# Softmax attention in a fused network: values' products one step later, joins in the next tile, mask after the scores

## The reference

```python
q = (h @ wq).reshape(B, S, NHEADS, HEAD_DIM)
k = (h @ wk).reshape(B, S, KVHEADS, HEAD_DIM)
v = (h @ wv).reshape(B, S, KVHEADS, HEAD_DIM)
q, k = _rope(q, k)
...
scores = jnp.einsum('bqhd,bkhd->bhqk', q, k) / np.float32(np.sqrt(HEAD_DIM))
scores = jnp.where(causal[None, None], scores, jnp.float32(-1e+30))
attn = jax.nn.softmax(scores, -1)
o = jnp.einsum('bhqk,bkhd->bqhd', attn, v).reshape(B, S, NHEADS * HEAD_DIM)
x = x + o @ wo
```

## Time and profile before

| what | us |
|---|---|
| median of three runs | 3796.96 |
| lowest and highest | 3794.91 and 3799.11 |
| the profiled execution | 3797.79 |
| its span, first to last instruction | 3795.8 |
| L0 attention, in the trace | 107.3 to 388.0 |
| L2 attention, first and second | 1045.1 to 1711.0 and 2482.1 to 3149.0 |

### The profile page before, as it was taken

One profiled execution on the slowest core, in us unless ns is written; L12 is line 12 of the kernel. 1 busy time (PEld: TensorE's weight loads), 2 busy tenths in 40 slices (PEclk: granted clock), 3 DMA queues, 4 the chain that ended last, 5 costly groups with the idle time before them and its releaser, 6 DMA issues. The chain is left out here.

```text
span 3795.8 us, 55139 instructions
## 1 busy us (share of the span) xinstructions
PE 3275.2 (86%) x16736; PEld 2538.9 (67%) x16736; DVE 2467.2 (65%) x4877; ACT 1972.1 (52%) x3957; POOL 1694.4 (45%) x1293
## 2 busy tenths in 40 slices
PE   5778699569888889988996899888889987998979
PEld 4566577138666666666884799756666666886767
DVE  4668545765578778885556565368778885555554
ACT  3777443333367667774333333267667774334333
POOL 1666221652276666762221454267666662221111
PEclk8999899899999999999998899899999999999989
DMA  2000131433211111103320000010111102332222
GB/s 76 23 30 2 50 116 62 125 109 113 76 26 25 28 31 30 27 7 110 108 93 21 6 1 1 29 39 25 25 28 30 30 9 93 113 105 86 70 95 75
DMA packets 81187, 204.07 MB, mean 54 GB/s; under 512 B 17179, under 2 KB 20379, under 8 KB 80662
## 3 DMA queue, kind: packets, MB, share of 16 engines
q1 hardware_dynamic: 80774, 200.74, 17.1%
q10 hardware_dynamic: 144, 0.07, 0.0%
HBM read 170.86 MB, written 4.69 MB: 46 GB/s over the span
## 5 line engine op out<-in xcount | busy, mean ns | idle before, releaser
L1252 POOL TENSOR_TENSOR probs<-probs,row_inverse 128x640 f32<-128x640 f32 (+7 forms) x640 | 739.0, 1159 | 514.5 <-DVE row_inverse L1278 503.0
L541 PE MATMUL psUp<-xnT_part,weights_part 128*128 128x512 f32 x3456 | 834.7, 391 | 3.3 <-DVE hidden L694 2.6
L541 PEld LDWEIGHTS psUp<-xnT_part,weights_part 128*128 128x128 f32 x3456 | 651.6, 189 | 141.7 <-issue 4.0
L518 POOL TENSOR_TENSOR weights_part<-weights,weights_part 128x768 fp32r<-128x768 f32 x136 | 250.9, 1848 | 1010.2 <-ACT weights_part L597 1010.2
L1266 DVE TENSOR_REDUCE neg_max<-psS 128x1 f32<-128x640 f32 (+7 forms) x640 | 477.0, 745 | 143.5 <-PE psS L1156 141.4
L1293 DVE TENSOR_TENSOR probsT_part<-psT,probsT_part 128x512 fp32r<-128x512 f32 (+1 forms) x960 | 501.9, 550 | 78.0 <-ACT probsT_part L1235 68.9
L1219 ACT ACTIVATE probs<-psS,neg_max 128x640 f32<-128x640 f32 (+7 forms) x640 | 475.6, 743 | 144.5 <-DVE neg_max L1266 127.7
L1235 ACT ACTIVATE probsT_part<-psT 128x512 fp32r<-128x512 f32 (+1 forms) x960 | 441.0, 491 | 174.0 <-PE psT L1168 164.4
L1189 PE MATMUL psO<-probsT_part,v_parts 128*128 128x512 f32 x1440 | 443.0, 423 | 73.7 <-DVE probsT_part L1293 72.7
L1152 PE MATMUL psS<-k_part,q_parts 128*128 128x512 f32 (+1 forms) x960 | 410.6, 428 | 80.3 <-ACT probs L1219 45.1
L1168 PE MATMUL psT<-ident,probs 128*128 128x128 f32 x2880 | 439.0, 276 | 43.1 <-DVE probsT_part L1293 39.3
(11 more groups left out here) (315 smaller groups left out, 4825.6 us busy)
## 6 DMA issues: line engine op xcount, KB each, us to landing
gates<-gate_rows SPq DMA_DIRECT2D x136, 512.0 KB, 4.0
weights<-in_l_ffn SPq DMA_DIRECT2D x148, 384.0 KB, 4.4
qk_swapped<-qk_raw SPq DMA_DIRECT2D x384, 64.0 KB, 2.0
bc_broadcast<-bc_rows SPq DMA_DIRECT2D x32, 512.0 KB, 4.5
w_group<-in_l_wgroup SPq DMA_DIRECT2D x16, 384.0 KB, 3.2
q_whole<-q_steps SPq DMA_DIRECT2D x32, 128.0 KB
w_o_group<-in_l_wo SPq DMA_DIRECT2D x16, 256.0 KB, 2.8
rope<-in_l_rope SPq DMA_DIRECT2D x2, 1024.0 KB, 5.3
```

Of the source, the lines that this page charges most:

```text
L518: nc.gpsimd.tensor_tensor(w[1][:, j, :], wt[:, j, :], w[0][:, j, :].bitcast(F32), ALU.subtract).then_inc(w_split, 1)
L541: last = nc.tensor.matmul(psU[:, u % 2, g, :], wp[:, j, g * D + k * P:g * D + (k + 1) * P], xp[:, k, cols(half)], start=n == 0, stop=n == ...
L1252: self.nc.gpsimd.tensor_tensor(self.p[:, n % 4, 0:w], self.p[:, n % 4, 0:w], self.rinv[:, at:at + 1].to_broadcast([P, w]), ALU.mult).then_ ...
```

## The change

The values' products move from a tile's steps 0, 1, 2 to its steps 1, 2, 3, and inside a step they stand between scores and turns instead of behind the turns. The join moves from step 3 of a tile to step 0 of the next one (the last tile's stays in step 30). The output jobs move two steps later (6, 10, 14, 18, 22, 26, 29, 31), with two buffers for `oT`; one projection moves from step 10 to 11, a rounding from 15 to 16, a split from 14 to 13, and the handling of the next group's values from steps 28 and 31 to 29 and 30 (GpSimd) and from 29 to 30 (VectorE). The product that adds the mask comes behind both score products of its block instead of between them. In L0 the roundings of steps 4 and 6 move to 13 and 14, the one of step 12 to 15, and the splits with them.

```diff
-    def joins(self, s):
-
-        return s == 30 or (s > 0 and s % 4 == 3 and s < 31)
+    def joined(self, s):
+
+        if s == self.UNITS - 2:
+            return NT - 1
+        return s // 4 - 1 if s > 0 and s % 4 == 0 else None
...
+                diagonal = b == qt // 4
                 nc.tensor.matmul(out[:, 0:w], queries, keys[0][:, b * HALF:b * HALF + w], start=True, stop=False)
-                if b == qt // 4:
-                    diagonal = out[:, qt % 4 * P:(qt % 4 + 1) * P]
-                    nc.tensor.matmul(diagonal, self.ident16[:], self.mask16[:], start=False, stop=False)
                 done = nc.tensor.matmul(out[:, 0:w], queries, keys[1][:, b * HALF:b * HALF + w],
-                                        start=False, stop=True)
+                                        start=False, stop=not diagonal)
+                if diagonal:
+                    done = nc.tensor.matmul(out[:, qt % 4 * P:(qt % 4 + 1) * P], self.ident16[:], self.mask16[:],
+                                            start=False, stop=True)
...
-            if s < 0 or r == 3:
+            if s < 0 or r == 0:
                 return
             blocks = self.blocks(s)
-            lo, hi = (r // 2 if r != 1 else 0, (r + 1) // 2) if blocks == 1 else (
-                r * blocks // 3, (r + 1) * blocks // 3)
+            lo, hi = (0 if r == 1 else 1, 1) if blocks == 1 else ((r - 1) * blocks // 3, r * blocks // 3)
...
             scores(g, s + 8, last)
+            values(g, s, last)
             turn(g, s + 4, last)
-            values(g, s, last)
             self.hooks.pe_step(pe, g, s, last)
...
-            if self.joins(s):
-                dve.wait_ge(self.shifted, NT * g + s // 4 + 1)
+            q = self.joined(s)
+            if q is not None:
+                dve.wait_ge(self.shifted, NT * g + q + 1)
...
-    PROJECT = (1, 3, 5, 7, 10, 13)
-    OUTPUT = (4, 8, 12, 16, 20, 24, 28, 31)
+    PROJECT = (1, 3, 5, 7, 11, 13)
+    OUTPUT = (6, 10, 14, 18, 22, 26, 29, 31)
+    ROUND_AT = {6: (0,), 8: (1,), 10: (2,), 12: (3,), 16: (4,), 18: (5,)}
+    SPLIT_AT = {7: 0, 13: 2, 15: 3, 22: 4, 24: 5}
...
-            if q:
-                self.wait_filled(dve, g, self.OUTPUT[q - 1], self.last)
+            if q > 1:
+                self.wait_filled(dve, g, self.OUTPUT[q - 2], self.last)
...
-        return self.nc.vector.tensor_tensor(self.oT[64 * half:64 * half + 64, :, :], first, second, ALU.add)
+        return self.nc.vector.tensor_tensor(self.oT[q % 2][64 * half:64 * half + 64, :, :], first, second, ALU.add)
...
-    ROUND_AT = {4: (0, 1), 6: (2,), 12: (3,), 20: (4,), 22: (5,)}
-    SPLIT_AT = {6: 0, 8: 2, 14: 3, 22: 4, 24: 5}
-    FIRST_KEYS_AT = 6
+    ROUND_AT = {13: (0, 1), 14: (2,), 15: (3,), 20: (4,), 22: (5,)}
+    SPLIT_AT = {14: 0, 15: 2, 16: 3, 22: 4, 24: 5}
+    FIRST_KEYS_AT = 14
```

More of the change, by code:

```diff
@@ L1279, in step @@
             maximum(g, s + 8, last)
-            if self.joins(s):
-                dve.wait_ge(self.shifted, NT * g + s // 4 + 1)
+            q = self.joined(s)
+            if q is not None:
+                dve.wait_ge(self.shifted, NT * g + q + 1)
                 for half in range(2):
                     pick = lambda ap: ap.rearrange("p (k h w) -> p k h w", h=2, w=P)[:, :, half, :]
-                    done = self.hooks.keep(dve, g, self.tile(s), half, pick(self.psO[0:self.dv, :]),
+                    done = self.hooks.keep(dve, g, self.tile(4 * q), half, pick(self.psO[0:self.dv, :]),
                                            pick(self.shift[:]))
@@ L1425, in dve_step @@
             self.split_first_keys(dve, g + 1)
-        if s == 29:
+        if s == 30:
             self.split_values(dve, g + 1, 0, slice(1, NT))
@@ L1449, in __init__ @@
         self.wo = s.sb("w_o_group", [P, KD, D])
-        self.oT = s.sb("oT", [P, KD, P])
+        self.oT = [s.sb(f"oT{i}", [P, KD, P]) for i in range(2)]
         self.rot = s.sb("rotated", [P, 2, 2, HALF])
@@ L1626, in pe_step @@
         for k in range(KD):
-            done = self.nc.tensor.matmul(self.share(s)[:, 0:D], self.oT[:, k, :], self.wo[:, k, :], start=k == 0,
+            done = self.nc.tensor.matmul(self.share(s)[:, 0:D], self.oT[j % 2][:, k, :], self.wo[:, k, :], start=k == 0,
                                          stop=k == KD - 1)
```

12 lines of the change are left out of this document (6 added, 6 removed).

## The result

The changed kernel takes **3884.8 us** (median of 4 runs, 3884.0 to 3885.8) against 3797.4 for the kernel before: a ratio of **1.0231, 95% interval 1.0213 to 1.0249**, some 87 us slower. The forecast was 3814 with a range from 3752 to 3852: the sign was right, the size was missed by 71 us.

What follows compares the result with a forecast made beforehand. TensorE was taken as the bound, VectorE a close second. 3797.8 + 22.4 (fourteen L2 groups) + 1.6 (last groups) - 15.7 (L0 stall) + 8.5 (L0 costs) = 3814.6 profiled, so 3814 us, range 3752 to 3852.

Steps and rivals of the forecast that it cites:

- The boundary, a wait of 2.05 for the join instead of 1.4: L2, step 17, where two tiles meet: TensorE's values' products wait 2.05 us for VectorE's join, before 1.4 for second parts.
- the 13.3 of the sum: One full L2 group after the change: TensorE's waits at all boundaries, with 0.8 spread over the rest, total 13.3 us.
- The 11.2 lost before: One L2 group before the change: TensorE's 7.4 us idle plus 3.9 for tails of about eleven waits.
- The mask: Mask product behind both scores: TensorE gains nothing, VectorE's maximum starts 0.07 us earlier, 0.5 a group at seven L2 boundaries.
- L0, the stall: L0 groups two and three: ScalarE's wait for keys from DRAM vanishes with roundings moved later, giving back 15.7 us.
- The crowded roundings: L0 steps 12 to 15, where ScalarE is nearly full: added roundings cost 1.7 us a group in three groups.
- L0's boundaries: Tile boundaries in L0 cost as in L2, about half as much for want of jobs: 0.8 us a group.
- The check by three pieces: The 32 steps of an L2 group worked through in three pieces: 2.5 us a group lost before the mask's 0.5.
- The slack: Rival, chance 0.26: waits of values' products and output jobs vanish, about 3 us a group come back elsewhere; 3750 us.
- the sign that I had set for it: Values' products' waits for the join in steps s%4 = 1 below 1 us would mean the slack works.
- VectorE falling behind for good: Rival, chance 0.09: two joins in the last tile's steps delay the next group, each losing 4 us, not 1.6; 3855.
- The clock: Rival, chance 0.02: clock falls at boundaries with scores, turns and a wait, some 2 us each, about 190 in all; 3990.

Runs made afterwards that it cites:

- before_late_jobs: Kernel before with the mask behind both score products, the L0 tables and the L2 tables of after (output jobs two steps later, two oT buffers): 3745.3 us, ratio 0.9869.

## Why the forecast was right in sign and wrong in size

*TensorE is the bound and VectorE a close second:* held. VectorE has the same work, and the time is lost because it gets it late.

*The boundary, a wait of 2.05 for the join instead of 1.4:* held at the place that I worked through (1.84 by its row, about 2.0 with the tail, and the join's end at 4.50 against 4.35). At the other boundaries the waits came out shorter than forecast: by the medians of fourteen groups 0.91 in step 5 (forecast 1.6), 0.82 in step 9 (1.4), 0.93 in step 13 (1.8), 1.0 in step 25 (1.5), 0.70 in step 29 (1.0), where about 0.27 of tail is to be added to each row. More small waits for exponentials made up for it: the 13 waits of the quiet group are 10.7, some 14.2 with tails, against the 13.3 of the sum. The output jobs' waits for second parts are gone, as said. The 11.2 lost before was worked out from eleven waits with tails of 0.35, but the earlier trace rows has eight, and the place worked through has a tail of 0.27 (1.41 less 1.14): that gives 9.5 lost before and a loss of 3.3 a group instead of 1.6 by the prediction's own rows.

*The order of turns and values: here the forecast failed.* I named what stands behind the waiting product ("the turns of unit 21 and the scores of unit 26, and ScalarE and VectorE wait for these") and gave it no price. In my working the turns came in only as cover of 0.22 that the wait loses. But 21 of 32 steps have values' products, two to six of 0.23 each, and in each of them the turns now start 0.5 to 1.4 later, wait or no wait. The runs give it a price of 60 to 65 us in this kernel: 18.5 and 19.6 of seven L2 groups (625.8 against 607.4, 622.5 against 602.9), 5.3 of each L0 group, and among these 7 of the 20 falls of the clock. With the order set back the kernel takes 3820, near the 3814, but that is not the sum come true: three L0 groups are then 14 us better than my figures for them (22.4 gained instead of 8.2) and fourteen L2 groups 24 worse (46 lost instead of 22).

*The products and the join one step later: the second step that failed, in size.* The sum had 1.6 a group for the boundaries of L2 and half of it in L0. With the order set back, the L2 groups with projections lose 5.5 each against before_late_jobs (77.4 in fourteen), and the L0 groups gain 1.2. The sum had no term for the projections of steps 3, 7 and 11, which now stand behind products and ahead of the join. The 46 are what the gains of the tables and the mask left of this.

*The mask: the size came out, the mechanism only in part.* I gave it no effect on TensorE and 0.5 a group through an earlier signal. In the kernel before it gives 10 us, which is 0.5 in each of 20 groups, but that is partly luck. It also saves TensorE 0.06 a unit, where I had taken the load that it exposes as equal at both places, and the run does not tell the two effects apart. In the kernel after the gain is not there.

*L0, the stall:* forecast 15.7, measured 16.5. *The crowded roundings:* forecast 1.7 a group, measured nothing, which was the lower bound of the term; ScalarE was nearly full in these steps, and what hid the roundings was not looked at. *L0's boundaries:* forecast 0.8 a group, measured 3.2 (69.54 against 66.39), by the order.

*The check by three pieces* gave 2.5 a group before the mask's 0.5, so 2.0, where I used 1.6. Neither had a term for the turns, but to stay with the lower figure had no reason in the rows.

*The jobs two steps later:* I counted their waits as gone and left it at that. The L2 tables, of which they are the main part, are worth 24 us, the largest gain in the change, and the sum gave 0.7 of waiting a group with its tail for it.

*The rivals.* The slack did not work, for the kernel is slower; but the sign that I had set for it was a poor one. Of the 42 waits of values' products in the seven groups from 1068.20, 35 are 0.7 to 1.1 and only the seven of step 17 are 1.6 to 1.9, and waits of 1 us and less did not make the group shorter. VectorE falling behind for good came nearest (3855, and 4 a group against measured 4.2 to 6.1), by another mechanism, since what is carried on is not the last tile's two joins but late turns in every tile. The clock did fall, with the chance that I had put at 0.02: I ruled it out because steps 20 to 23 before, with 30 turns, ran at 1.00, and did not ask what the same turns do behind a wait. The price of a fall was near (about 1.7 against 2), but there were 20 of them and not one at every boundary: some 30 us more than before in both L2 stages instead of 190.

## What to carry to other kernels

Where one engine feeds several chains in each step, first list for each instruction who waits for it, and put work that nobody waits for (here the values' products) last; moving it ahead of the head of a chain makes the engines that follow late, and that cost 60 to 140 us here although their busy shares show room. Price a change of order by every step in which it holds, not by the one boundary that it is meant for. Before moving work into a step, look at which other job already stands there and who reads its result. And take a change with several parts apart: here three of them (the mask, the L0 tables, the L2 tables) were worth 46 us together, while the others (products and joins one step later, TensorE's order) cost 133 to 140.

## What the runs showed of the hardware that I had not expected

- The granted clock can fall to the lower level behind waits of only 0.60 and 0.92 us in one step: it did so in step 13 in eight of fourteen groups and not in the six others. With such waits filled by products that are thrown away, eight falls in 537 us became two.
- A short bfloat16 product (the mask, 128 columns) is dearer between two score products (0.36 for a block of 256 columns) than behind both (0.28 to 0.30).
- A stretch of TensorE can take 19.4 us more of work and be 3.0 us shorter.
